# A two-layer gated cross-attention block on one core: mixes moved behind the turns, GpSimd's side work placed anew, query stacks signalled by head

## The reference

```
x = x + tanh(g_xattn[0]) * attention0(layernorm(x), ctx)   # 16 heads of depth 8, mask of batch 0
x = x + tanh(g_ffn[0])   * ffn0(layernorm(x))              # Hadamard, 4-bit rows, ternary weight
x = x + tanh(g_xattn[1]) * attention1(layernorm(x), ctx)   # 16 heads of depth 64, mask per batch
x = x + tanh(g_ffn[1])   * ffn1(layernorm(x))              # 32 experts, top 4, and a shared one
attention: softmax(mask(q k^T / sqrt(depth))) v, then an output projection with bias
```

## Time and profile before

| | |
|---|---|
| median of three runs | 268.72 us (267.73 to 848.29) |
| the profiled execution | 268.18 us, of which the trace spans 266.4 us |
| TensorE busy | 251.8 us (94%) |
| VectorE busy | 210.2 us (79%) |
| ScalarE busy | 188.5 us (71%) |
| GpSimd busy | 181.1 us (68%) |
| granted TensorE clock | full in all 40 slices |

### The profile page before, as it was taken

One profiled execution on the slowest core, in us unless ns is written; L12 is line 12 of the kernel. 1 busy time (PEld: TensorE's weight loads), 2 busy tenths in 40 slices (PEclk: granted clock), 3 DMA queues, 4 the chain that ended last, 5 costly groups with the idle time before them and its releaser, 6 DMA issues.

```text
span 266.4 us, 6698 instructions
## 1 busy us (share of the span) xinstructions
PE 251.8 (94%) x1899; PEld 198.7 (75%) x1899; DVE 210.2 (79%) x654; ACT 188.5 (71%) x451; POOL 181.1 (68%) x272
## 2 busy tenths in 40 slices
PE   7997999999789999999999999999999999998994
PEld 5664667767557777778777888777887768998993
DVE  3899998999999896789668877777898624995863
ACT  2487898998799777857776767686787654545652
POOL 5667999985889765746844485439767795946660
PEclk9999999999999999999999999999999999999999
DMA  6457453300015854645484766756552051213610
GB/s 194 158 163 260 170 179 101 121 0 4 1 37 126 183 108 106 140 91 122 119 218 114 190 175 185 186 131 159 156 134 62 6 159 39 75 47 100 183 61 20
DMA packets 25475, 31.86 MB, mean 120 GB/s; under 512 B 4000, under 2 KB 18144, under 8 KB 25312
## 3 DMA queue, kind: packets, MB, share of 16 engines
q1 hardware_dynamic: 25008, 31.23, 43.8%
q10 hardware_dynamic: 432, 0.22, 0.3%
HBM read 14.32 MB, written 2.42 MB: 63 GB/s over the span
## 4 chain that ended last, share of the span: by engine, by line
PE 68%; DVE 14%; issue 8%; POOL 6%; ACT 3%; DVEq 0%; ACTq 0%; POOLq 0%
PE bank L1319 16%; PE bank L1492 14%; PE bank L1324 6%; PE bank L1326 6%; PE bank L1325 6%; PE bank L1454 5%; PE bank L1455 5%; DVE masked L986 4%; POOL probs L637 3%; PE bank L1507 3%; DVE probsT L1003 2%; PE bank L1515 1%; PE bank L1572 1%; PE bank L1574 1%; PE bank L1573 1%
## 5 line engine op out<-in xcount | busy, mean ns | idle before, releaser
L637 POOL TENSOR_SCALAR probs<-probs,rsum 128x512 f32<-128x512 f32 x128 | 87.8, 692 | 49.3 <-DVE rsum L995 48.3
L783 ACT ACTIVATE probs<-masked,neg_max 128x512 f32<-128x512 f32 x128 | 91.7, 718 | 11.8 <-DVE neg_max L986 8.8
L1319 PE MATMUL bank<-ident,probs 128*128 128x128 f32 x512 | 78.5, 276 | 2.5 <-DVE probsT L1003 1.2
L1319 PEld LDWEIGHTS bank<-ident,probs 128*128 128x128 f32 x512 | 58.7, 141 | 19.1 <-issue 10.3
L986 DVE CUSTOM_DVE_ANT_0 masked<-bank,mask 128x512 f32<-128x512 f32 x64 | 43.7, 684 | 15.2 <-PE bank L1455 14.6
L792 ACT ACTIVATE probsT<-bank 128x512 f32<-128x512 f32 x74 | 43.6, 589 | 15.2 <-PE bank L1319 14.8
L1492 PE MATMUL bank<-probsT,val 128*32 128x256 f32 (+1 forms) x512 | 46.6, 384 | 0.0
L1003 DVE COPY probsT<-bank 128x512 f32<-128x512 f32 x54 | 36.7, 680 | 8.8 <-PE bank L1319 8.5
L986 DVE CUSTOM_DVE_ANT_0 masked<-bank,shared 128x512 f32<-128x512 f32 x64 | 43.3, 678 | 0.1
L1492 PEld LDWEIGHTS bank<-probsT,val 128*32 128x32 f32 (+1 forms) x512 | 24.4, 123 | 18.0 <-issue 4.8
L1448 PE MATMUL bank<-parts 128*128 128x512 f32 x64 | 31.1, 486 | 1.6 <-DVE neg_max L986 1.3
(11 more groups left out here) (254 smaller groups left out, 517.9 us busy)
## 6 DMA issues: line engine op xcount, KB each, us to landing
k_both<-k_low SPq DMA_DIRECT2D x32, 128.0 KB, 2.9
k_both<-k_high SPq DMA_DIRECT2D x32, 128.0 KB, 2.9
q<-q_split SPq DMA_DIRECT2D x32, 128.0 KB, 2.4
probsT<-staged_gate SPq DMA_DIRECT2D x32, 128.0 KB, 3.0
q<-q_split SPq DMA_DIRECT2D x32, 64.0 KB, 2.1
parts<-staged_k SPq DMA_DIRECT2D x7, 256.0 KB, 2.8
w_flat<-in_w SPq DMA_DIRECT2D x1, 1536.0 KB, 8.1
staged_q<-q_split SPq DMA_DIRECT2D x4, 256.0 KB, 2.7
```

The lines of the kernel that those rows point to most:

```text
L637: pool.tensor_scalar(p, p, rsum[:, u % NCOL:u % NCOL + 1], 1.0, ALU.mult, ALU.mult).then_inc(normed, 1)
L783: act.activation(probs[:, u % NP, :], masked[:, u % NS, :], ACT.Exp, scale=-1.0, bias=neg_max[:, c:c + 1], accum_out=sums[:, c:c + 1]).the ...
L1319: ins = pe.transpose(dst[0:rows, t * P:t * P + P], src, ident[:, :])
```

## The change

1. First-layer mixes go behind the turn of their step; second-layer mixes stay ahead of it.
2. The job q 8 goes behind the turn of step 52; q 9 goes from step 56 to 57.
3. In every q job, the two products that need only the high part of x come first, then the wait for its low part, then the third product.
4. `v0` of batch 1 goes from step 17 to 21, `turn_fw` from 21 to 23.
5. GpSimd: the two memsets go from steps 8 and 10 to 19 and 30; the bias scaling from 10 to 11; the bias of batch 1 from 16 to 39; the masks from 12, 14, 16, 18 to 16, 26, 35, 41; the values of batch 1 from 20, 22, 29, 37 to 28 (two) and 37 (two); two context splits from 22 and 32 to 23 and 33.
6. Unit 42 is copied by ScalarE instead of VectorE.
7. The stack semaphores are split by head; `stack_q` sends a head's high part as soon as that is ready, and waits for the low part only ahead of the first low DMA. Scores wait for their head's alone.

```diff
-        plan.setdefault(k.first - early - (12 if k.m < 10 else 11), []).append(("q", k.m))
+        plan.setdefault(k.first - early - (12 if k.m == 8 else 11), []).append(("q", k.m))
     for n, name in enumerate(("kn", "qn", "v0")):
-        plan.setdefault(LN01_AT + 7 + 2 * n, []).append((name, 1))
+        plan.setdefault(LN01_AT + (7, 9, 15)[n], []).append((name, 1))
...
-    plan.setdefault(21, []).append(("turn_fw",))
+    plan.setdefault(23, []).append(("turn_fw",))
...
-MORE_ON_ACT = (36, 46, 48, 68, 70, 78, 80, 102, 110, 112)
+MORE_ON_ACT = (36, 42, 46, 48, 68, 70, 78, 80, 102, 110, 112)
...
-SPLIT_AT = dict(zip((22, 32, 42, 49, 54, 58, 62, 66, 70, 74, 77, 80),
+SPLIT_AT = dict(zip((23, 33, 42, 49, 54, 58, 62, 66, 70, 74, 77, 80),
...
-VALUES_AT = {4: (0, (0, 1, 2, 3)), 20: (1, (0,)), 22: (1, (1,)), 29: (1, (2,)), 37: (1, (3,))}
+MASKS_AT = (16, 26, 35, 41)
+VALUES_AT = {4: (0, (0, 1, 2, 3)), 28: (1, (0, 1)), 37: (1, (2, 3))}
...
             def stack_q(k):
-                sp.wait_ge(*freed(("q", k.m)))
+                sp.wait_ge(high_ready, HIGHS["q", k.m])
                 sp.wait_ge(scored, BLOCKS[k.m - NKQ].end)
                 for h in range(2):
                     sp.dma_start(q1[own[h], s, h, :, :].bitcast(F32),
-                                 q1_split[own[h], i, 0, :].bitcast(F32).unsqueeze(1).to_broadcast([64, 2, SQ])).then_inc(q_stacked[s], 16)
+                                 q1_split[own[h], i, 0, :].bitcast(F32).unsqueeze(1).to_broadcast([64, 2, SQ])).then_inc(q_stacked[s][h], 16)
+                    if h == 0:
+                        sp.wait_ge(*freed(("q", k.m)))
...
-                if t in (8, 10):
-                    publish_late(pool.memset(q1_high[:, :, t // 10, :].bitcast(F32), 0.0))
-                if t in (10, 43):
-                    scale_bias(int(t > 10))
+                if t in (19, 30):
+                    publish_late(pool.memset(q1_high[:, :, t // 30, :].bitcast(F32), 0.0))
+                if t in (11, 43):
+                    scale_bias(int(t > 11))
                 for b in range(B):
-                    if t == (13, 16)[b]:
+                    if t == (13, 39)[b]:
                         add_bias(0, b)
...
                         if name == "q":
+                            pe.wait_ge(x1_high_ready, k.b + 1)
+                            c = slice(k.b * SQ, k.b * SQ + SQ)
+                            pe.matmul(job_bank[:, 0:SQ], low, x1_high[:, c], start=True, stop=False)
+                            pe.matmul(job_bank[:, 0:SQ], high, x1_high[:, c], start=False, stop=False)
                             pe.wait_ge(*freed(("ln", 2, k.b)))
-                            c = slice(k.b * SQ, k.b * SQ + SQ)
-                            ins = three(job_bank[:, 0:SQ], high, low, x1_high[:, c], x1_low[:, c])
+                            ins = pe.matmul(job_bank[:, 0:SQ], high, x1_low[:, c], start=False, stop=True)
...
                 for j in PLAN.get(t, ()):
-                    job(j)
-                for k in BLOCKS:
+                    if j != ("q", 8):
+                        job(j)
+                for k in BLOCKS[8:]:
                     if t == k.mix_at:
                         mix(k)
-                    if t == k.out_at and k.layer:
+                    if t == k.out_at:
                         project_out(k)
                 if 0 <= t < TOTAL:
                     turn(t)
+                if ("q", 8) in PLAN.get(t, ()):
+                    job(("q", 8))
+                for k in BLOCKS[:8]:
+                    if t == k.mix_at:
+                        mix(k)
```

More of the change, by code:

```diff
@@ L428, in build @@
         x1_high_ready = sem("x1_high_ready")
-        k_stacked = [sem(f"k_stacked{i}") for i in range(NKQ)]
-        q_stacked = [sem(f"q_stacked{i}") for i in range(NKQ)]
+        k_stacked = [[sem(f"k_stacked{i}_{h}") for h in range(2)] for i in range(NKQ)]
+        q_stacked = [[sem(f"q_stacked{i}_{h}") for h in range(2)] for i in range(NKQ)]
         q0_ready = sem("q0_ready")
@@ L554, in stack_k @@
                 for h in range(2):
-                    sp.dma_start(k1_both[own[h], s, h, :].bitcast(F32), k1_low[own[h], i, :].bitcast(F32)).then_inc(k_stacked[s], 16)
-                    sp.dma_start(k1_both[own[1 - h], s, h, :].bitcast(F32), k1_high[own[h], s, :].bitcast(F32)).then_inc(k_stacked[s], 16)
+                    sp.dma_start(k1_both[own[h], s, h, :].bitcast(F32), k1_low[own[h], i, :].bitcast(F32)).then_inc(k_stacked[s][h], 16)
+                    sp.dma_start(k1_both[own[1 - h], s, h, :].bitcast(F32), k1_high[own[h], s, :].bitcast(F32)).then_inc(k_stacked[s][h], 16)
             def stack_q(k):
                 i, s = k.m % 2, k.m % NKQ
-                sp.wait_ge(*freed(("q", k.m)))
+                sp.wait_ge(high_ready, HIGHS["q", k.m])
                 sp.wait_ge(scored, BLOCKS[k.m - NKQ].end)
@@ L563, in stack_q @@
                     sp.dma_start(q1[own[h], s, h, :, :].bitcast(F32),
-                                 q1_split[own[h], i, 0, :].bitcast(F32).unsqueeze(1).to_broadcast([64, 2, SQ])).then_inc(q_stacked[s], 16)
+                                 q1_split[own[h], i, 0, :].bitcast(F32).unsqueeze(1).to_broadcast([64, 2, SQ])).then_inc(q_stacked[s][h], 16)
+                    if h == 0:
+                        sp.wait_ge(*freed(("q", k.m)))
                     sp.dma_start(q1_both[own[1 - h], s, h, :].bitcast(F32),
-                                 q1_split[own[h], i, 1, :].bitcast(F32)).then_inc(q_stacked[s], 16)
+                                 q1_split[own[h], i, 1, :].bitcast(F32)).then_inc(q_stacked[s][h], 16)
             for t in sorted(PLAN):
@@ L667, in split_weights @@
                     for m in (22, 23):
-                        pool.wait_ge((k_stacked if n < 14 else q_stacked)[m % NKQ], 64 * turns_of_stack(m))
+                        for h in range(2):
+                            pool.wait_ge((k_stacked if n < 14 else q_stacked)[m % NKQ][h], 32 * turns_of_stack(m))
                 else:
@@ L748, in _ @@
                     rstd_of(3, 0)
-                if t >= 12 and t % 2 == 0 and t < 12 + 2 * B * NQ:
+                if t in MASKS_AT:
                     pool.wait_ge(ld["m1"], 16)
-                    b, i = divmod((t - 12) // 2, NQ)
+                    b, i = divmod(MASKS_AT.index(t), NQ)
                     pool.tensor_scalar(mask1[:, b, i, :], m1_u8[:, b, i, :], -FAR, 0.0, ALU.mult,
@@ L831, in job @@
                         else:
-                            act.wait_ge(q_stacked[(k.m - 2) % NKQ], 64 * turns_of_stack(k.m - 2))
+                            for h in range(2):
+                                act.wait_ge(q_stacked[(k.m - 2) % NKQ][h], 32 * turns_of_stack(k.m - 2))
                         high = q1_split[:, i, 0, :]
@@ L1050, in job @@
                         else:
-                            dve.wait_ge(k_stacked[(k.m - 2) % NKQ], 64 * turns_of_stack(k.m - 2))
+                            for h in range(2):
+                                dve.wait_ge(k_stacked[(k.m - 2) % NKQ][h], 32 * turns_of_stack(k.m - 2))
                         low, bank_in, bias, high = k1_low[:, i, :], job_bank[:, :], bk1, k1_high[:, k.m % NKQ, :]
@@ L1056, in job @@
                         else:
-                            dve.wait_ge(q_stacked[(k.m - 2) % NKQ], 64 * turns_of_stack(k.m - 2))
+                            for h in range(2):
+                                dve.wait_ge(q_stacked[(k.m - 2) % NKQ][h], 32 * turns_of_stack(k.m - 2))
                         low, bank_in, bias, high = q1_split[:, i, 1, :], job_bank[:, 0:SQ], bq1, q1_split[:, i, 0, :]
@@ L1451, in scores @@
                     s = k.m % NKQ
[L1452 to L1453 removed]
+                    pe.wait_ge(k_stacked[s][h], 32 * turns_of_stack(k.m))
+                    pe.wait_ge(q_stacked[s][h], 32 * turns_of_stack(k.m))
                     pe.matmul(dst, q1_high[:, s, h, q], k1_high[:, s, :], start=True, stop=False)
```

2 lines of the change are left out of this document (removed).

## The result

| | before | after |
|---|---|---|
| median of 13 runs each | 267.87 us | 269.32 us |
| profiled execution | 268.18 us | 269.4 us |
| its span, mean granted clock | 266.4 us, 1.000 | 267.7 us, 0.992 |

The ratio after to before is 1.0042 with a 95% interval from 1.0025 to 1.0059. The change makes the kernel 0.4% slower, where I had forecast 0.4% faster. The time lies in the range; the sign doesn't follow the forecast. One execution of each kernel was far slower (848.29 and 406.1 us) and is left out of the ratio.

What follows compares the result with a forecast made beforehand. VectorE and ScalarE in turn bound the first layer, TensorE the second. The terms -1.37 - 0.33 - 0.35 - 0.16 + 1.13 = -1.08 us on 268.18 us gave 267.1 us; range 265.0 to 269.5, with 0.50 on 266.2 to 268.0.

Steps and rivals of the forecast that it cites:

- k 10's wait: With q 9 in step 57, k 10 waits for its bank and starts 1.24 us later; cost 1.13 us.
- rival (b): ScalarE keeps the first layer to its time, so the kernel is slower: 269.1, up to 269.5 us; chance 0.11.
- step 18: First layer: the mask of unit 25 comes 1.96 us earlier, `v0`'s copy returns 0.59; gain 1.37 us.
- step 26: First layer: with the turn ahead of the mix, VectorE's stall moves from copy to next mask; gain 0.33 us.
- step 34: First layer: the same gain from the turn going ahead of the mix as in step 26; 0.35 us.
- GpSimd beside the feed-forward: GpSimd's side work moved into later steps was priced at 0, with GpSimd's slack as cover.
- unit 42 to ScalarE: At 68.85 us the copy takes 0.59 us from VectorE, but ScalarE has little gap behind; gain 0.16 us.
- Rival (d): GpSimd's moved bias and mask meet VectorE's feed-forward instructions, twice 0.6 us; end 268.3 us; chance 0.06.
- The norms as a condition: First layer: a turn can go first only if its unit is normed, so GpSimd's moves are the condition.
- rival (c): Steps 18 to 34: the turn is not normed in time and the mix waits behind it; 268.3 us; chance 0.06.
- q 8 and the stacks at 0: Second layer: q 8's new place, its product order (bounds 0 and 0.25 us) and stacks by head each gain 0.
- Rival (a): Second layer: k 10's wait is hidden, all 2.2 us of gains remain plus extras; 265.4 us; chance 0.22.

Runs made afterwards that it cites:

- e3: The kernel before with only q 9 moved from step 56 to 57; 271.17 us, ratio 1.0107 to the kernel before.
- e1: The change with q 9 back in step 56; 267.06 us, ratio 0.9966 to the kernel before.
- e4: The change with three matmuls of 256 columns, result unread, ahead of k 10's wait; 268.37 us, ratio 1.0005 to the kernel before.
- e7: The kernel before with only GpSimd's side work, `v0` and `turn_fw` where the change has them; 267.55 us, ratio 0.9993.
- e10: e5 with the mixes of blocks 3 and 7 (steps 34 and 66) ahead of their turns again; 266.54 us, ratio 0.9938 to the kernel before.
- e5: e1 with GpSimd's last values moved from step 37 to 46 and its last mask from 41 to 45; 266.23 us, ratio 0.9940.
- e9: e5 with unit 42 copied by VectorE again; 267.05 us, ratio 0.9965 to the kernel before.
- e6: The kernel before with only the first-layer mixes moved behind their turns; 269.5 us, ratio 1.0054 to the kernel before.
- e8: e1 with the edits to the second layer's queries and stacks undone; 267.18 us, ratio 0.9976 to the kernel before.
- e11: The kernel before with only `v0` moved from step 17 to 21, and two GpSimd values that need it to 28; 269.53 us, ratio 1.0059.
- e2: The change with k 10 moved from step 58 to 59; 267.65 us, ratio 0.9981 to the kernel before.

## Why the prediction was wrong

**The step that failed is the price of k 10's wait.** The mechanism of the wait was right in each part: VectorE's order, the bank, the gap of "1.5 us or more" (1.67), the releaser. Its term of the sum was +1.13 us, and it measured +2.9 (from -0.90 at unit 62 to +2.00 at the end; e3 alone +2.91). The start of k 10 comes 1.3 us later, close to what I took. What I left out is the lower clock that TensorE was granted after the idle stretch: 1.5 us on the 3.2 us of work behind it. e1 (no wait) and e4 (a filled wait) show both parts. Nothing of before showed it: the clock was 1.000 there in spite of idle stretches of up to 1.25 us. The forecast for the clock was, silently, zero. The executions of the change bear it out from outside. Five had a mean granted clock of 0.998 or more and took 267.89 to 268.99 us; seven had 0.994 or less and took 269.22 to 269.66. So the clock doesn't fall in each execution, and where it holds, the change still costs about 0.5 us more than it gives: the middle one of the five is 268.42, against 267.87 before. e4, with the wait but not the slow stretch, says the same (+0.45 by the ruler).

Had only this term been right (2.9 for 1.13), the forecast would have been 268.18 - 2.05 - 0.16 + 2.9 = 268.9. The gains fell short too: they came to 0.90 us by unit 62 and not to 2.2. Both together are 3.1 us on the ruler; the profiled time is only 2.3 above the forecast because x was loaded 0.79 us earlier in that execution. That the time still lies in the range is luck: the range's upper end, 269.5, was that of rival (b), a ScalarE that holds the first layer back, and this is not what happened.

| term | forecast | measured (ruler) | units |
|---|---|---|---|
| step 18 with `v0`'s copy | -1.37 | -1.06 | to 28 |
| step 26 | -0.33 | -0.31 | 28 to 33 |
| step 34 | -0.35 | +0.10 | 33 to 43 |
| GpSimd beside the feed-forward | 0 | +0.70 | 43 to 47 |
| unit 42 to ScalarE | -0.16 | -0.33 | 47 to 62 |
| q 9 to step 57, with k 10 | +1.13 | +2.90 | 62 to 127 |
| sum | -1.08 | +2.00 | |

**Step 18** was 0.31 short: unit 25 came 1.65 us early instead of 1.96, then 0.59 for the copy as forecast. ScalarE was not the brake: its exponential of unit 24 starts at 38.24 and follows without idle time, where I had listed under 0.3. TensorE's timeline of the change has the turn of unit 18 and the mix:

```profile
35.91 0.63 PE L1326 MATMUL bank<-ident,probs 128*128 128x128 f32 x4
36.47 1.93 PE L1502 MATMUL bank<-probsT,val 128*32 128x256 f32 x32
```

By the ruler (plus 0.79) the turn starts at 36.70 and the mix at 37.26, where I had 36.5 and 36.9: 0.2 lost ahead of the turn, 0.16 since the way from turn to mix takes 0.56 us and not 0.4. The turn starts 0.14 us behind the end of ScalarE's copy of unit 15, the event that I had named; the sizes were off and not the mechanism. Nor was it mainly the new order that won this step (e7).

**Step 26** held, to 0.02 us. Unit 32's mask, where I had listed 1.4 us, came 1.04 early, and unit 47's, where I had listed 2.0, 0.57. **Step 34** reached -0.19 by unit 41 and lost it at unit 43, where ScalarE's result copy comes later behind the later mix; I had that as a line of rival (b) and not in the sum. e10 shows the remedy (-1.36 kept), worth 0.17 at the end.

**Rival (d) came true** beside the main miss, with 0.70 us where its upper price was twice 0.6. I gave it 0.06 and treated it as an alternative; it was a term of the sum, which had the moved work at 0 because of GpSimd's slack. One of the two pieces that I had named, the mask of step 41, hit an instruction; the other, the bias of step 39, did not, and the values of step 37 did by way of a norm. It cost 0.6 at the end (e5 against e1). The Trainium skill (SBUF — State Buffer, "SBUF: two separate sides") says that whichever of the two engines starts first holds the shared pair for its whole instruction, for some kinds of VectorE's instructions. The trace agrees: GpSimd's started first (58.91 against 59.03, 63.26 against 63.40), and the short instruction ended with GpSimd's and not by its own size. I had looked for instructions of VectorE of some length to be hit, and found ones of 0.17 us.

**Unit 42** gave 0.36 (e5 against e9), twice my 0.16. I had priced it at one idle stretch of ScalarE.

**The norms as a condition** stood as the prediction had them: e6 shows the mechanism of rival (c), +1.31 us, with a turn that waits for a norm behind a split. What I hadn't seen is that the condition is worth more than what it permits (e7).

**q 8 and the stacks at 0** was right for the change and wrong for the kernel. q 8 still waits for L1039 (L1034 before) in the change, as listed; the gain of 0.09 lies within the bound of 0.25. With k 10's wait gone the stack is worth about 0.7 us (e8). That the wait hides this gain in the change is as argued; no run has the change with the old stacks.

**Rival (a)** had its condition wrong. The idle time that was to hide the wait isn't there, and e1 without any wait at k 10 ends only 0.84 us earlier by the ruler.

The forecast and its range leaned on a single small difference, 2.2 won and 1.1 lost, each uncertain by more than what was left. 0.50 for the forecast, and 0.11 for slower, was too sure of the sign.

## What to carry to other kernels

When a job is moved one step later, look at the job that follows it in the same bank, not only at the one for which it waited: k 10 behind q 9, `turn_fw` behind `v0` in e11 and q 10 behind k 10 in e2 each waited, for 1.67, 1.21 and 0.67 us, until a job just ahead of them was copied. A wait on TensorE can have a second price, the clock behind it; read the granted clock in short stretches behind each new gap (here wait and clock together cost 2.9 us, about twice the wait's own 1.3). When several edits go in together, take each out or in alone: here the one that gave the change its name was the smaller part of its gain. Side work that is moved to where its engine has slack can stretch another engine's small instructions, so place it by what the other engine is doing then and not by the slack alone.

## What the runs showed of the hardware

**The clock.** In the profiled execution of the change TensorE was busy 0.64 us of 84.0 to 86.3, with one idle stretch of 1.67 us, and got a mean clock of 0.56 over the next 3.7 us and 1.00 from 90 us on. In e3 idle stretches of 0.49 and 1.09 us with two matmuls between them were followed by 0.64 over 4 us. The same kernel kept its clock in some executions and not in others (five and seven of the change, one and five of e3). In the kernel before, TensorE's timeline has an idle stretch of 1.25 us behind which the page's clock stays full in each slice:

```profile
68.39 0.41 PE L1319 MATMUL bank<-ident,xq 128*128 128x128 f32 x2 [1.25 <-DVE xq L1101]
```

So 1.25 us at one place was followed by no lower clock, and 1.09 at another was. The length of one gap doesn't decide alone; what does was not settled. A filler of 1.46 us in the same wait kept the clock at 1.00 (e4), and the kernel with it ends 1.55 us earlier by the ruler.

**GpSimd against VectorE.** An instruction of VectorE on 128x2 elements, SBUF to SBUF, took 0.61 us instead of 0.17, and another 0.48 instead of 0.16, each until GpSimd's instruction beside it ended. Not every small instruction is hit: beside the same norm at 58.91 the two BATCH_NORM_AGGREGATE of VectorE (58.74, 128x2 from 128x6) took 0.25 us together, as in e5, and a SCALAR_TENSOR_TENSOR of 128x2 that writes a bank (62.75) took 0.15 beside another norm. Larger instructions that read from a bank (masks of 0.68, copies of 0.67 us) kept their usual length in the rows shown, with GpSimd's norms going on beside them.
